# Two conditioned attention blocks, 32 sequences on one core: another order of the same pieces on all engines, with other PSUM banks

## What is computed

```python
# block 0: "efficient" attention, 8 heads of 32
xn = ln(x)
q = softmax(heads(xn @ Wq + bq), over the 32 features)
k = softmax(heads(xn @ Wk + bk + mask), over the 256 tokens)
v = (xn @ Wv + bv) * mask
att = einsum('bnhd,bnhl->bhdl', k, v)            # 32 x 32 per head
y = einsum('bnhd,bhdl->bnhl', q, att)
scale, shift = split(silu(emb) @ W_emb + b_emb)
x1 = x + silu(ln(y) * (1 + scale) + shift) @ W_out + b_out
# block 1: softmax attention, 16 heads of 16, over 256 x 256 scores
q, k, v = heads(ln(x1) @ W + b)
y = softmax(q @ k.T + mask) @ v
out = x1 + silu(ln(y) * (1 + scale1) + shift1) @ W_out1 + b_out1
```

## Time and profile before

| what | value |
|---|---|
| median of 3 runs | 822.89 us (822.42 to 824.58) |
| span of the profiled execution | 824.9 us |
| instructions | 27262 |
| TensorE busy | 797.7 us, 97% (9407 matmuls) |
| weight loads | 572.0 us, 69% |
| VectorE busy | 735.6 us, 89% |
| ScalarE busy | 704.5 us, 85% |
| GpSimd busy | 688.7 us, 83% |

### The profile page before, as it was taken

How to read it: one execution, slowest core, us unless ns; L and a number is a source line. 1 busy time by engine, 2 the same in 40 slices (tenths; PEclk the granted TensorE clock), 3 DMA queues, 4 the chain that set the end, 5 groups by cost and what they waited for, 6 DMA issues and landing times.

```text
span 824.9 us, 27262 instructions
## 1 busy us (share of the span) xinstructions
PE 797.7 (97%) x9407; PEld 572.0 (69%) x9407; DVE 735.6 (89%) x1488; ACT 704.5 (85%) x1658; POOL 688.7 (83%) x1021
## 2 busy tenths in 40 slices
PE   7998999999999999999999999999999999999995
PEld 3575776777777777677777777777777777666643
DVE  6899999998989999989898889989898989898962
ACT  2366678999898998898898998889989999999995
POOL 8579899999878999789898999888889987896423
PEclk9899999999999999999999999999999999999998
DMA  7522355354344443334545543353454433444411
GB/s 184 153 40 67 96 140 133 81 119 112 86 108 109 105 126 102 98 90 98 122 107 136 121 98 84 84 134 106 110 122 109 109 88 80 99 104 128 116 34 39
DMA packets 149276, 86.11 MB, mean 104 GB/s; under 512 B 87404, under 2 KB 141802, under 8 KB 149130
## 3 DMA queue, kind: packets, MB, share of 16 engines
q1 hardware_dynamic: 149140, 84.36, 42.4%
HBM read 39.64 MB, written 25.80 MB: 79 GB/s over the span
## 4 chain that ended last, share of the span: by engine, by line
PE 41%; issue 12%; POOL 9%; DVE 9%; DMA 2%; SPq 1%; ACT 1%; POOLq 0%; DVEq 0%; ACTq 0%
PE banks L708 11%; PE banks L861 7%; PE banks L716 5%; PE banks L835 4%; PE banks L848 4%; PE banks L723 3%; DVE NM L1308 3%; PE banks L738 2%; PE banks L787 2%; PE banks L871 2%; DVE st L1199 1%; POOL YN L2015 1%; POOL rs L2011 1%; POOL ZHL L2036 1%; POOL SH L2088 1%
## 5 line engine op out<-in xcount | busy, mean ns | idle before, releaser
L1308 DVE TENSOR_REDUCE NM<-banks 128x4 f32<-128x1024 f32 x256 | 306.4, 1212 | 25.1 <-PE banks L835 24.0
L1807 ACT ACTIVATE wraw<-banks 128x1024 f32<-128x1024 f32 x154 | 155.9, 1034 | 8.0 <-PE banks L848 7.3
L2011 POOL TENSOR_TENSOR rs<-ve,nhalf 128x2 f32<-128x2 f32 x128 | 89.7, 703 | 31.6 <-ACT ve L1682 31.4
L1807 ACT ACTIVATE PX<-banks 128x1024 f32<-128x1024 f32 x102 | 103.5, 1035 | 8.6 <-PE banks L848 7.3
L2088 POOL TENSOR_TENSOR SH<-ST,SH 128x512 f16<-128x512 f32 x64 | 74.4, 1164 | 31.4 <-ACT SH L1771 31.4
L708 PE MATMUL banks<-wo,SH 128*128 128x256 f16 x768 | 94.9, 274 | 4.5 <-POOL SH L2088 4.4
L708 PE MATMUL banks<-wv,ZT 128*128 128x256 f16 x768 | 93.5, 273 | 1.4 <-DVE wv L1404 0.5
L835 PE MATMUL banks<-SK,SQ 51*128 51x256 f16 x1024 | 92.5, 272 | 0.8 <-ACT wemb L1815 0.3
L848 PE MATMUL banks<-SQ,SK 53*128 53x256 f16 x1024 | 90.6, 271 | 2.1 <-DVE NM L1308 1.0
L2036 POOL TENSOR_TENSOR ZHL<-Z,ZHL 128x256 f16<-128x256 f32 x128 | 87.5, 704 | 2.6
L861 PE MATMUL banks<-wraw,V 128*32 128x256 f32 x1232 | 87.2, 385 | 0.8 <-DVE NM L1308 0.8
(11 more groups left out here) (186 smaller groups left out, 1879.5 us busy)
## 6 DMA issues: line engine op xcount, KB each, us to landing
scr<-AB SPq DMA_DIRECT2D x64, 256.0 KB, 2.6
X<-in_x_dram SPq DMA_DIRECT2D x32, 256.0 KB, 2.8
SK<-scr SPq DMA_DIRECT2D x64, 128.0 KB, 2.9
SQ<-scr SPq DMA_DIRECT2D x64, 128.0 KB, 2.7
out_dram<-wemb SPq DMA_DIRECT2D x32, 256.0 KB, 2.5
SK<-scr SPq DMA_DIRECT2D x64, 64.0 KB, 2.9
SQ<-scr SPq DMA_DIRECT2D x64, 64.0 KB, 2.7
wemb<-in_L_cond_W_emb_dram SPq DMA_DIRECT2D x1, 1024.0 KB, 5.5
```

The source lines that it names most:

```text
L1308: V.tensor_reduce(NMe[:, c, :, 2 * g:2 * g + 2], banks[:, n:n + 2, :].rearrange("p a (h m) -> p a h m", m=T), AX.X, ALU.max, negate=True). ...
L1807: A.activation(px(v % 5), banks[:, n:n + 2, :].rearrange("p a n -> p (a n)"), ACT.Exp, scale=r_uu).then_inc(S["exp"])
L2011: G.tensor_tensor(rs[:, b % 2, l, :], ve[:, b % 2, l, :], nhalf[:, :], ALU.pow).then_inc(S[f"r{l}"])
```

## The change

The functions are the same, to the letter. What differs is the written order of every engine and of SP's queue, the tables BANK and FREED, and SETUP. TensorE, VectorE, ScalarE, GpSimd and SP each have the same pieces as before, as often as before. Since the tables are shorter, a line of the new file has a number lower by about 10 to 19 (L835 is L825 now, L2056 is L2037).

```diff
--- before.py
+++ after.py
 BANK = {
...
-    "gr0": "00402404646460424404200042262666",
+    "gr0": "22420622204240462620642664424204",
...
 FREED = {
...
-        "o1p+q1:6 kt:7+x1:4 exp:5 exp:11 exp:21 exp:27 o:3+kt:12 max:56 vt:9+kt:14 exp:60 exp:69 exp:76 "
...
+        "kt:5+o1p qt:6+max:8 exp:5 exp:11 max:32 exp:28 max:48 exp:44 exp:51 exp:61 x1:13+qt:15 exp:76 ke:18+o:9 "
...
 SETUP = {
...
     "DVE": (
-        "hz mb0 w0m mx_w0 o0m csl w0p mx_o0 p3 wl_k0 wl_q0 o0p wl_v0 wl_o0 f0m mx_f0 w1m film0 mx_w1 w1p "
+        "hz mb0 w0m mx_w0 csl o0m w0p mx_o0 wl_k0 p3 wl_q0 wl_v0 f0m mx_f0 o0p w1m film0 mx_w1 wl_o0 w1p bm o1m mx_b "
...
         @block.sync
-            ld_m(); ld_w0(); x_in(0); x_in(1); ld_r(); ld_o0(); ld_c(); x_in(2); fd(); mbd0(); ld_f0(); z0T(0)
-            am(0); am(1); x_in(3); am(2); ld_f1(); x_in(4); am(3); z0T(1); fill_k(); ld_w1(); ld_o1(); z0T(2)
+            ld_m(); x_in(0); ld_w0(); x_in(1); ld_r(); ld_c(); ld_o0(); mbd0(); ld_f0(); ld_o1(); am(0); x_in(2)
+            ld_f1(); fd(); z0T(0); x_in(3); am(1); am(2); ld_w1(); z0T(1); x_in(4); am(3); z0T(2); z0T(3); am(4)
...
         @block.tensor
-            hot(); pm(); tr_w0(); row3(); ar_w0(); tr_o0(); cnd_t(); bb0(); ar_o0(); bb1(); k0(0); q0(0); fx0()
-            v0(0); ktT(0); fm0(); q0(1); att(0); qtT(0); k0(1); tr_f0(); y0(0); v0(1); k0(2); ar_f0(); ktT(1)
+            hot(); pm(); tr_w0(); bb0(); ar_w0(); bb1(); tr_o0(); cnd_t(); row3(); fx0(); k0(0); q0(0); q0(1); fm0()
+            v0(0); k0(1); tr_f0(); ktT(0); qtT(0); v0(1); att(0); q0(2); ar_o0(); y0(0); ktT(1); ar_f0(); v0(2); q0(3)
...
-            cols(16, 6); pv(16, 4); att(23); pv(16, 5); cols(16, 7); rows(18, 3); y0(22); y1T(15); rows(18, 4)
-            rows(18, 5); ty(16, 0); y0T(21); k0(24); pv(16, 6); pv(16, 7); cols(17, 0); rows(18, 6); cols(17, 1)
+            y1T(15); y0(22); q0(24); y0T(21); rows(18, 4); rows(18, 5); pv(16, 6); pv(16, 7); att(23); k0(24)
...
         @block.scalar
-            n0(0); th(); n0(1); csT_(); pa(); wh_k0(); wh_q0(); ru(); wh_v0(); bc1(); bc0(); mc(); n0(2); ke(0)
+            n0(0); th(); n0(1); mc(); wh_k0(); csT_(); pa(); n0(2); wh_v0(); wh_q0(); n0(3); bc1(); bc0(); fy0(); ru()
...
```

More of the change, by code:

```diff
@@ new lines @@
+    "ga_f0": "6",
+    "gt_w1": "0",
+    "gy0T": "10567523004312670112313360226026",
+    "grw": "7",
+    "ga_w1": "4",
+    "go0": "17763550101440637504342712416235",
+    "gcol": "3",
+    "gt_b": "3",
+    "gbb2": "1",
+    "ga_b": "3",
+    "gfx1": "7",
+    "gt_o1": "3",
+    "gk1": "67426410113217261140231030401247",
+    "gfm1": "7",
+    "gq1": "01011501005267200051547340010644",
+    "ga_o1": "3",
+    "gv1": "50704214122656603134211610743160",
+    "gr0": "22420622204240462620642664424204",
@@ L92 @@
+    "gy1T": "31361100511710565750536732642454",
+    "go1": "43016330567100211043010421612455",
 }
@@ L263 @@
     "PE": (
-        "hot pm tr_w0 row3 ar_w0 tr_o0 cnd bb0 ar_o0 bb1 fx0 fm0 tr_f0 ar_f0 tr_w1 ar_w1 rw col tr_b tr_o1 "
-        "ar_b fx1 ar_o1 fm1 tr_f1 bb2 ar_f1 ").split(),
+        "hot pm tr_w0 bb0 ar_w0 bb1 tr_o0 cnd row3 fx0 fm0 tr_f0 ar_o0 ar_f0 tr_w1 rw ar_w1 col tr_b bb2 ar_b fx1 "
+        "tr_o1 fm1 ar_o1 tr_f1 ar_f1 ").split(),
     "DVE": (
-        "hz mb0 w0m mx_w0 o0m csl w0p mx_o0 p3 wl_k0 wl_q0 o0p wl_v0 wl_o0 f0m mx_f0 w1m film0 mx_w1 w1p "
-        "wl_k1 bm o1m mx_b fcs wl_q1 mx_o1 o1p f1m wl_v1 wl_o1 mx_f1 film1 ").split(),
+        "hz mb0 w0m mx_w0 csl o0m w0p mx_o0 wl_k0 p3 wl_q0 wl_v0 f0m mx_f0 o0p w1m film0 mx_w1 wl_o0 w1p bm o1m mx_b "
+        "wl_k1 fcs wl_q1 wl_v1 f1m mx_o1 o1p mx_f1 film1 wl_o1 ").split(),
     "ACT": (
-        "th csT pa wh_k0 wh_q0 wh_v0 bc1 bc0 mc wh_o0 fy0 wh_k1 perm wh_v1 wh_q1 fy1 wh_o1 bc2 ").split(),
+        "th mc wh_k0 csT pa wh_v0 wh_q0 bc1 bc0 fy0 wh_o0 perm wh_k1 wh_v1 fy1 wh_q1 bc2 wh_o1 ").split(),
     "POOL": (
-        "nmz cst v1z mb1 ").split(),
+        "cst v1z mb1 nmz ").split(),
 }
@@ new lines, in _ @@
+            pv(8, 0); pv(8, 1); pv(8, 2); pv(8, 3); pv(8, 4); cols(8, 5); cols(8, 6); rows(10, 2); y0(14); y1T(7)
+            cols(8, 7); rows(10, 3); att(15); pv(8, 5); pv(8, 6); pv(8, 7); rows(10, 4); rows(10, 5); y0T(13)
+            ty(8, 0); k0(16); ty(8, 1); v1p(11); v0(16); cols(9, 0); cols(9, 1); rows(10, 6); q0(16); o1(7)
+            cols(9, 2); rows(10, 7); cols(9, 3); k1p(12); o0(13); cols(9, 4); rows(11, 0); rows(11, 1); qtT(15)
+            ktT(16); q1p(12); rows(11, 2); cols(9, 5); pv(9, 0); pv(9, 1); pv(9, 2); pv(9, 3); pv(9, 4); pv(9, 5)
@@ new lines, in _ @@
+            rows(12, 5); rows(12, 6); pv(10, 6); pv(10, 7); att(17); y1T(9); k0(18); q0(18); v1p(13); v0(18)
+            ty(10, 0); cols(11, 1); cols(11, 2); rows(12, 7); k1p(14); ktT(18); ty(10, 1); o1(9); q1p(14); rows(13, 0)
+            rows(13, 1); cols(11, 3); o0(15); qtT(17); cols(11, 4); pv(11, 0); pv(11, 1); pv(11, 2); pv(11, 3)
+            cols(11, 5); rows(13, 2); cols(11, 6); att(18); pv(11, 4); pv(11, 5); rows(13, 3); rows(13, 4)
+            cols(11, 7); y0(17); ty(11, 0); y1T(10); k0(19); y0T(16); v0(19); v1p(14); cols(12, 0); rows(13, 5)
@@ new lines, in _ @@
+            pv(18, 7); o1(17); k1p(22); ty(18, 1); rows(21, 0); cols(19, 2); o0(23); cols(19, 3); rows(21, 1); qtT(25)
+            q1p(22); v1p(21); ktT(26); rows(21, 2); cols(19, 4); pv(19, 0); pv(19, 1); pv(19, 2); pv(19, 3)
+            cols(19, 5); rows(21, 3); cols(19, 6); y0(25); rows(21, 4); cols(19, 7); pv(19, 4); att(26); pv(19, 5)
+            pv(19, 6); pv(19, 7); rows(21, 5); cols(20, 0); ty(19, 0); y0T(24); y1T(18); q0(27); v0(27); k0(27)
+            rows(21, 6); rows(21, 7); cols(20, 1); q1p(23); ty(19, 1); qtT(26); o1(18); k1p(23); rows(22, 0)
@@ new lines, in _ @@
+            cols(22, 6); ktT(29); y0(28); cols(22, 7); rows(24, 4); rows(24, 5); pv(22, 4); pv(22, 5); att(29)
+            pv(22, 6); pv(22, 7); rows(24, 6); cols(23, 0); y0T(27); y1T(21); rows(24, 7); cols(23, 1); ty(22, 0)
+            v0(30); k0(30); ty(22, 1); qtT(29); q0(30); v1p(25); k1p(26); o1(21); cols(23, 2); cols(23, 3)
+            rows(25, 0); q1p(26); o0(27); ktT(30); rows(25, 1); cols(23, 4); pv(23, 0); pv(23, 1); cols(23, 5)
+            rows(25, 2); cols(23, 6); pv(23, 2); pv(23, 3); pv(23, 4); pv(23, 5); att(30); rows(25, 3); cols(23, 7)
@@ new lines, in _ @@
+            rows(25, 4); y0(29); y1T(22); ty(23, 0); pv(23, 6); pv(23, 7); rows(25, 5); cols(24, 0); v0(31); y0T(28)
+            rows(25, 6); cols(24, 1); ty(23, 1); k0(31); q0(31); k1p(27); q1p(27); rows(25, 7); cols(24, 2)
+            cols(24, 3); o1(22); cols(24, 4); rows(26, 0); o0(28); qtT(30); ktT(31); cols(24, 5); rows(26, 1)
+            pv(24, 0); pv(24, 1); pv(24, 2); att(31); pv(24, 3); rows(26, 2); cols(24, 6); v1p(26); cols(24, 7)
+            rows(26, 3); y0(30); y1T(23); y0T(29); rows(26, 4); rows(26, 5); pv(24, 4); pv(24, 5); pv(24, 6)
```

949 lines of the change are left out of this document (446 added, 503 removed), and 171 rows, old and new, of the table FREED.

## The result

The changed kernel takes 842.07 us (median of 4 runs, 840.46 to 843.87), the kernel before 823.2 in the same comparison: 1.022 times as long, 95% interval 1.0198 to 1.0244. 818.0 was forecast.

What follows compares the result with a forecast made beforehand. TensorE's own stream was taken to bound 117.5 to 780 us, VectorE the stretch before. 824.9 - 2.4 (shapes) - 2.5 (opening) = 820.0, less 2.0 because the profiled execution stood above the median: 818.0, range 814.5 to 822.5.

Steps and rivals of the forecast that it cites:

- The counts and prices of shapes: TensorE from cols(0,0) on: changes of tile shape fall from 482 to 466, saving 2.4 us (1.5 to 3.0).
- The opening: Start, before 117.5 us: less waiting of VectorE, a gain of 2.5 us, between a loss of 3.0 and a gain of 3.0.
- the first x ahead of the weights on SyncE's queue: Opening, SyncE's queue: first x loads issued before weights, one of the reorderings behind the 2.5 us gain.
- what I cost at nothing: Moves priced at zero, among them ld_o1's two loads ahead of x_in(2) on SyncE's queue; uncovered, one landing.
- The lower end, 3.0: Opening: if TensorE's clock drops all the same, fx0 takes 7.4 us and k0(0) comes later, a loss of 3.0 us.
- the wait for s0(2): Opening, VectorE: s0(2) wants its x ahead of wl_k0; one of the new waits covered by half a microsecond left out.
- The long part: 117.5 to 780 us, bound by TensorE's stream: apart from shapes, -1.5 to +2 us kept for changed waits.
- Banks cost nothing but through their waits: Long part: slightly sooner bank reuse priced at zero, with -1.5 to +2 us kept for waits.
- The slower rival: Long part: VectorE's maxima come late for rows and cols; 0.35 us of waiting a batch gives 827.8 us; chance 0.06.
- I had 4.9: Whole kernel: the forecast gain, 2.4 us from fewer shape changes plus 2.5 us from the opening.

Runs made afterwards that it cites:

- Run 1: Changed kernel with SyncE's opening loads reordered: third x ahead of the conditioning matrix, second block's loads behind the second transposing DMA; 838.7 us, ratio 1.015.
- run 2: Changed kernel with one TensorE piece moved: q0(1) behind fm0(0) and v0(0) instead of ahead of them; 838.5 us, ratio 1.014.
- run 4: Kernel before with the changed kernel's SyncE queue order up to z0T(3), all else its own; 826.7 against 825.5 us, ratio 1.001.
- run 3: Changed kernel with 89 of SyncE's 398 steps moved from nr(1) on (about 125 us), ready transfers ahead of waiting ones; 837.8 us, ratio 1.015.
- run 5: Changed kernel with SyncE's queue reordered both in the opening and in the long part; 834.0 us, ratio 1.010.
- run 7: On top of run 5, VectorE, ScalarE and GpSimd reordered from 125 us on (127 pieces, 11 SyncE steps), TensorE's order kept; 822.4 us, ratio 0.996.
- run 10: Run 7 with SyncE's queue put back to the changed kernel's order from x_in(5) on, opening loads still mended; 836.7 us, ratio 1.016.
- run 8: Like run 7, but VectorE, ScalarE, GpSimd and SyncE rearranged from 40 us on; 820.8 us, ratio 0.995 to the kernel before.
- run 11: Run 8 rearranged a second time by traces, 118 steps moved, 30 of them on TensorE; 818.0 us, ratio 0.991 to the kernel before.

## Why the prediction was wrong

**The counts and prices of shapes were right.** 2.4 us forecast, 2.5 by the sum of prices. The trace bears out the 0.10 us per departure once more. From the 128 cycles of a drain in the Trainium skill (TensorE: Matmul & The Clock Gate, What happens when you issue a matmul) the estimate was 0.05 us; the trace has twice that.

**The opening: -2.5 forecast, +7.0 measured.** The step that failed is "the first x ahead of the weights on SyncE's queue" taken as a gain, with ld_o1 ahead of x_in(2) under "what I cost at nothing". The queue was read for what it moved ahead, not for what it put behind: the 1 MB matrix and two loads of a later block stood ahead of the third x, which was issued 4.5 us later and landed after 7.0 us instead of 3.6. The lower end, 3.0, knew only the clock. And the wait for s0(2), which I named, was priced at part of half a microsecond; the row says 2.75, and wk's scaling was queued behind it. q0(1), moved up to q0(0), isn't among the waits I named, and waited 3.21 us. Run 1 mends the late transfers and run 2 the one early reader, and run 4 shows that late transfers alone cost nothing.

**The long part: -1.5 to +2 forecast, +11.7 measured.** The failing step is "Banks cost nothing but through their waits", with at most 2 us of loss kept for them. I had measured the distances on TensorE's own stream only. The 398 steps of SyncE's queue I looked at in the opening alone, though every batch passes through it with twelve steps, in strict order. DMAs that ended waits made 6.9 of the 11.5 us between 120 and 780; another order of the queue took away 4.6 (run 3), and another order of the other engines on top 10.7 (run 5 to run 7).

**The slower rival had the wrong mechanism.** It made VectorE's maxima late: their waits went from 3.6 to 4.0 us. I gave it 0.06 at 827.8 because one wait of 0.35 us a batch seemed much; it was 0.4 a batch, from many small ones.

**Why the order looked good.** Replayed with the typical duration of each kind of piece and transfer, the changed order takes 806.9 us and the old one 812.3: by such numbers it is 5.4 better, and I had 4.9. Replayed with each piece's own duration as its trace has it, they take 842.3 and 823.2, as on the chip within 2 us. So the loss sits in the departures from the typical. If only SyncE's departures (issues and landings) are put in, the changed order goes from 806.9 to 827.8, the old one from 812.3 to 814.4. These are estimates worked out from the traces, and their size hangs on what is taken as typical. A coarser replay, with the median of each kind of piece over both traces, gives 807.4 and 808.9, only 1.5 us apart. There SyncE's departures alone add 14.8 and 1.6 us, and VectorE's alone 10.4 and 3.6. So the direction stands, and VectorE's departures have a part in it as well. Runs 3, 7 and 10 are what was measured.

On the queue, the row of nr(19) shows that a step waits its turn behind others' issues whatever its own data does. The Trainium skill (DMA: Bandwidth & Descriptors, Anatomy of one DMA) says that a DMA engine never waits on a semaphore; the wait is on the issuing sequencer. By that rule one step that isn't ready holds all behind it, and the trace agrees: in the kernel before, am(3) waits for k0(0) and goes out at 26.00, and z0T(1) behind it, whose data was ready at 21.17, at 26.43. The same section of the Trainium skill has a fixed cost of about 2.0 us, roughly constant, for DMAs that GpSimd issues; these are issued by SyncE, and the small transposing DMA of the maxima landed after 2.3 us at the median and 4.3 at most in the changed kernel.

**Open.** Which transfers disturb which was not tried, nor a second queue for the loads, nor s0(2) moved by itself. Why the waiting behind cols(0,0) grew by 2.4 us when the opening was mended, and why the old order had so few late transfers, isn't known from the traces.

## What to carry to other kernels

When an order is changed, read every in-order queue for what each step now stands behind, the DMA queue first, and ask of each reader that moves up whether its transfer will have landed. A plan made with typical durations promised 5 us and lost 19. The same TensorE order, with the pieces around it placed by the durations of its own traces, took 0.995 of the kernel before (run 8), and with 30 of its own pieces moved too 0.991, the fastest of all. Give the old kernel the same treatment before you credit the change. Undo the parts one by one, on the old kernel too: an edit that costs 5 us in one order can cost nothing in the other.

## What was not expected of the hardware

- Departures from the typical durations repeat as long as the order stays nearly the same. Over the same pieces, the changed kernel and run 2 correlate at 0.94 for VectorE's intervals between starts, 0.97 for ScalarE's, 0.86 for GpSimd's, 0.57 for the landing times of DMAs. Between the kernel before and the changed one these are 0.24, 0.01, 0.19 and 0.11. A new order draws new ones. The figures leave out intervals in which the next piece waited; with these in, the two orders correlate at 0.2 to 0.5.
- An issue on SyncE's queue mostly takes 0.25 to 0.5 us, a transposing one 1.24. While the 1 MB matrices of the opening were under way, single issues took up to 2.97 us, and a load of 256 KB landed after 7.0 us instead of about 3.
- The low clock moves even where the order does not. Runs 1 and 10 have the same order on every engine up to 142 us: in run 10 the granted clock was 0.5 from 72.0 to 78.8 us and cols(0,0) came at 118.7, in run 1 it was full there and cols(0,0) came at 117.0. The changed kernel and run 3, alike up to 142 us too, have 124.5 and 122.7. In run 11 it was at its lower level nowhere between the first microseconds and 800 us.
